# A layer norm beside a stream of scattered writes: four VectorE operations of 128x1792, each written as seven of 128x256

## The reference, cut to what matters

```
x0  = first layer: out[r] = sum over edges (r, c) of x[c] * norm(r, c)
x   = layernorm(x + x0)                       # the norm in question
xw  = einsum('ni,rih->rnh', x, W)             # 8 relations, for the second layer
layernorm(v) = (v - mean(v)) / sqrt(var(v) + 1e-5)   over the 64 features
```

## Time and profile before

| | us |
|---|---|
| median of 3 runs | 6556.67 |
| lowest, highest | 6533.79, 6564.7 |
| the profiled execution | 6601.09 |
| its span | 6599.3 |
| share of the span that DVE is busy, whole program | 35% |
| share for POOL | 43% |

### The profile page before, as it was taken

One profiled execution on the slowest core, in us unless ns is written; L12 is line 12 of the kernel. 1 busy time (PEld: TensorE's weight loads), 2 busy tenths in 40 slices (PEclk: granted clock), 3 DMA queues, 4 the chain that ended last, 5 costly groups with the idle time before them and its releaser, 6 DMA issues. The chain is left out here.

```text
span 6599.3 us, 74663 instructions
## 1 busy us (share of the span) xinstructions
PE 4016.7 (61%) x20669; PEld 3196.6 (48%) x20669; DVE 2306.5 (35%) x4709; ACT 1303.5 (20%) x2394; POOL 2863.7 (43%) x2799
## 2 busy tenths in 40 slices
PE   2333362567666642666189888878971668616687
PEld 2112111566422222666189555676751558416686
DVE  6444491234565620114511011243540113401136
ACT  0000000001343410001111222344530001300025
POOL 0655506664366666660400566000126661266602
PEclk9656575555666765555555888999985555755569
DMA  2000041111455531113633333363431112511136
GB/s 96 2 2 2 11 139 32 39 44 41 154 211 205 214 107 29 45 46 133 241 103 106 90 86 89 125 185 142 180 123 25 45 45 84 198 29 45 45 114 227
DMA packets 236073, 639.42 MB, mean 97 GB/s; under 512 B 75772, under 2 KB 77025, under 8 KB 220247
## 3 DMA queue, kind: packets, MB, share of 16 engines
q1 hardware_dynamic: 95223, 478.17, 20.1%
q0 software_dynamic: 87808, 66.01, 5.5%
q10 hardware_dynamic: 52704, 90.93, 3.7%
HBM read 324.53 MB, written 323.19 MB: 98 GB/s over the span
## 5 line engine op out<-in xcount | busy, mean ns | idle before, releaser
L1020 PE MATMUL e_ring<-e_msgs,e_hot 128*128 x6272 | 1413.7, 414 | 1081.2 <-issue 1064.8
L1020 PEld LDWEIGHTS e_ring<-e_msgs,e_hot 128*128 128x128 f32 x6272 | 1381.2, 329 | 1116.6 <-issue 1116.3
L898 POOL DMA_INDIRECT e_msgs<-y,index_D x784 | 741.5, 946 | 633.6 <-issue 453.9
L950 DVE TENSOR_TENSOR e_hot<-e_nodes,keys_D 128x2048 f32<-128x2048 f32 x147 | 336.9, 2292 | 1610.1 <-remote 884.5
L1166 POOL DMA_INDIRECT m_far<-x,index_S x392 | 373.9, 954 | 543.1 <-PE m_p_t L72 356.5
L1058 ACT COPY e_stage<-e_ring 128x512 f32<-128x512 f32 x196 | 114.9, 586 | 2458.3 <-remote 1434.6
L634 POOL DMA_INDIRECT list_D<-d_place,d_target x392 | 448.3, 1144 | 340.6 <-DVEq L588 225.2
L634 POOL DMA_INDIRECT list_S<-s_place,s_target x392 | 387.0, 987 | 436.3 <-DVEq L588 320.9
L898 POOL DMA_INDIRECT e_msgs<-y,index_S x392 | 402.7, 1027 | 364.3 <-DVE index_S L936 177.2
L898 POOL DMA_INDIRECT e_msgs<-x_by_relation,index_D x392 | 374.2, 955 | 214.6 <-issue 112.7
L1320 PE MATMUL m_ring<-m_region,m_hot 128*128 x1568 | 343.3, 423 | 60.5 <-issue 60.5
(11 more groups left out here) (361 smaller groups left out, 6329.6 us busy)
## 6 DMA issues: line engine op xcount, KB each, us to landing
x_by_relation<-d_stage SPq DMA_DIRECT2D x98, 1024.0 KB
agg<-e_stage ACTq DMA_DIRECT2D x196, 256.0 KB
n_in<-agg SPq DMA_DIRECT2D x42, 896.0 KB, 5.5
n_in<-x SPq DMA_DIRECT2D x42, 896.0 KB, 5.3
x<-n_out SPq DMA_DIRECT2D x28, 896.0 KB, 3.6
m_keyrow<-keys_by_step SPq DMA_DIRECT2D x49, 512.0 KB
messages<-m_region SPq DMA_DIRECT2D x98, 256.0 KB
m_region<-messages SPq DMA_DIRECT2D x49, 512.0 KB, 4.0
```

The costliest lines, as they stand in the source:

```text
L898: pool.indirect_dma_start(out=msgs[:, (i % HELD) * D:(i % HELD + 1) * D], out_offset=None, in_=source, in_offset=bass.IndirectOffsetOnAxis ...
L950: nc.vector.tensor_tensor(hot[g % 2][:, :, :], bc(nodes[:, 0:P].unsqueeze(1), [P, GS, P]), bc(order["keys"][:, g * GS:(g + 1) * GS].unsque ...
L1020: mm = nc.tensor.matmul(ring[:, bass.ds(bucket, D)], hot[g % 2][:, k, :], msgs[:, bass.ds(tile, D)], start=False, stop=False, skip_group_c ...
```

## The change

Each of the four operations of the norm with two tensor operands runs over all 28 nodes of a partition. It is now seven instructions, each over four nodes (128x256). The waits stand before the first, the signal is on the last. The two reductions, `hots`, the copies and everything on other engines stay as they are.

```diff
+        pieces = [slice(n * QUAD, (n + 1) * QUAD) for n in range(UQ)]
...
-                    nc.vector.tensor_tensor(value[:, :, :], got_a[h][:, :, :],
-                                            bc(K["dis"][:, c * CH:(c + 1) * CH].unsqueeze(2), [P, CH, D]), ALU.mult
-                                            ).then_inc(s_v, 1)
+                    for p in pieces:
+                        op = nc.vector.tensor_tensor(value[:, p, :], got_a[h][:, p, :],
+                                                     bc(K["dis"][:, c * CH:(c + 1) * CH][:, p].unsqueeze(2), [P, QUAD, D]),
+                                                     ALU.mult)
+                    op.then_inc(s_v, 1)
...
-                    nc.vector.tensor_tensor(value[:, :, :], value[:, :, :], got_x[h][:, :, :], ALU.add
-                                            ).then_inc(s_value, 1)
+                    for p in pieces:
+                        op = nc.vector.tensor_tensor(value[:, p, :], value[:, p, :], got_x[h][:, p, :], ALU.add)
+                    op.then_inc(s_value, 1)
...
-                    nc.vector.tensor_tensor(cent[:, :, :], value[:, :, :], bc(mean[:, :].unsqueeze(2), [P, CH, D]),
-                                            ALU.subtract).then_inc(s_c, 1)
+                    for p in pieces:
+                        op = nc.vector.tensor_tensor(cent[:, p, :], value[:, p, :],
+                                                     bc(mean[:, p].unsqueeze(2), [P, QUAD, D]), ALU.subtract)
+                    op.then_inc(s_c, 1)
...
-                    nc.vector.tensor_tensor(result[h][:, :, :], cent[:, :, :],
-                                            bc(rstd[:, :].unsqueeze(2), [P, CH, D]), ALU.mult).then_inc(s_done, 1)
+                    for p in pieces:
+                        op = nc.vector.tensor_tensor(result[h][:, p, :], cent[:, p, :],
+                                                     bc(rstd[:, p].unsqueeze(2), [P, QUAD, D]), ALU.mult)
+                    op.then_inc(s_done, 1)
```

## The result

| | before | changed |
|---|---|---|
| median, us | 6560.68 (6533.79 to 6590.12, 4 runs) | 6636.97 (6614.68 to 6641.81, 4 runs) |
| ratio of the runs, changed to before, 95% interval | | 1.0116 [1.009, 1.0143] |
| the profiled execution: its span | 6599.3 | 6612.9 |

A forecast was written before the change was run, and what follows sets the result against it. No engine was full on average; VectorE was on the path in some two fifths of the steps, GpSimd ahead. Chunk 0's 1.6 us plus 10.4 us for steps 0 and 1 made 12.0, on 6556.67: 6569 us, range 6546 to 6592.

The forecast's parts named there:

- the one on the puts: GpSimd's puts, held less, gain 35 us; all falls into its wait for L588, so nothing counted, bounds nothing and 35.
- step 6: Before each chunk's loose half: VectorE's 7.34 us idle before its copy hides the 0.40; nothing counted, at most 5.2 us.
- The line for a piece: VectorE start to start: 1.04 ns an element plus 0.067 us an instruction, so 0.333 us for 256 elements.
- 22.5 us more on VectorE: Seven pieces take 0.40 us more than one operation, over 56 operations; 12.0 us of it counted on the path.
- The sum's lower end, 0: Low end of the 12.0 us on the path, if the DMA would have held the stage anyway; upper end 22.4.
- chunk 0: First chunk, almost wholly in the dense head of 32 us: 4 x 0.40 = 1.6 us, all paid.
- Rival 1: A put takes the port from VectorE's next piece for 0.84 us: 50 us more, 6619 us; chance 0.04.
- Rival 2: No overlap on VectorE: each piece costs its whole 0.42 us, 30 us on the path, 6587 us; chance 0.05.
- Rival 5: VectorE doesn't let go between pieces, so puts wait for the whole series; same time as forecast, sharing its 0.68.
- Rival 3: Added VectorE time vanishes because DMA and stores set the dense half: 0 to 2 us, 6557 us; chance 0.18.
- Rival 4: GpSimd's puts pace something without a profile: up to 35 us back against 12, 6534 us; chance 0.05.
- the tail of the forecast: The forecast's own slow end, over 6589 us, one part of the 0.07 given to slower by over 0.5%.

The follow-up runs named there:

- e1: The kernel before, with GpSimd waiting for all 14 targets before its first put, so the norm runs without puts beside it; span 6859.7 us, one run.
- e4: The kernel before with each of the four operations replaced by a one-operand reduction of the same length, which holds no put; 6637.8 us, ratio 1.0124.
- e2: The changed kernel, with GpSimd waiting for all 14 targets before its first put, so no puts run beside the norm; span 6875.9 us, one run.
- e7: The kernel before with every eighth put waiting until the put ahead of it has landed; ratio to before 1.0065.
- e3: The kernel before with six one-column memsets ahead of each of the 56 whole operations, puts held as before; 6559.04 us, ratio 1.0005.

## Why the prediction was wrong

The step that failed is the one on the puts: "All of it falls into its wait for L588 ... I take nothing for the gain. Bounds: nothing, and 35 us". It bounds what an unheld stream of puts does by what it could give. That it could take something had no bound, though the rows asked for one: the "remote" waits behind step 6 were set down as a cause "on TensorE's side", and used as a cover, without asking what made a matmul's reader wait 7 us and more for something recorded as finished. e1 shows that they come from the puts: none is left until the puts begin. e4 shows that with the holds gone and nothing added they grow from 404 to 552 us and the whole loss of 1.2% is there; in the changed kernel they are 536.

- What bounds the kernel: that GpSimd is ahead of VectorE was right in the rows, and the conclusion that its speed is free was wrong. On the chips with late signals the puts' stream is what slows the norm, 31.7 to 45.7 us a chunk.
- The line for a piece: 0.333 us from start to start, right (2.44 us a series). 22.5 us more on VectorE, of which 12 on the path: the runs show 7 us where no put runs beside it (e1, e2). Beside the puts no run has it alone, but e4, which has none of it, loses as much as the change (1.0124 against 1.0116). It is not where the time went. The sum's lower end, 0, also leaves out the 1.6 us of chunk 0 that the list calls paid.
- The puts' durations: mean forecast about 1050, measured 1016; maximum under 2100, measured 2320, and it is the 1372 comparison that holds it (started at 1775.58, 0.10 us ahead of the put). GpSimd's wait for L588: 30 us more forecast, 108.7 measured. This row alone would have told that the forecast was off.
- Rival 1 (a put takes the port from a piece) is refuted: no piece over 429 ns. The Trainium skill (SBUF — State Buffer, Who interferes with whom) calls the pair an exclusive lock. No row here shows a put that keeps it from a piece. Rival 2 is refuted by 2.44 against 2.94. The Trainium skill's (N+151)/0.96 (VectorE: DVE Perf Modes, The TRN2 errata) gives by estimate 424 ns for a piece. The trace agrees with 419, but the pieces overlap, 0.333 us from start to start. Rival 5 is refuted by the puts' mean.
- Rival 3 (hidden whole) had no term for a loss from the puts; as to VectorE's added work e4 speaks for it. Rival 4 (the puts pace something, up to 35 us back) had 0.05, and is what happens on the other chip, where the 45 us of hold come back as 40.
- The chance of slower by over 0.5% was put at 0.07, and stood on rivals 1 and 2 and the tail of the forecast; none of them has the cause that the runs showed.

Not settled: what makes TensorE's signals late. Measured are these: a rest at every eighth put leaves 50 us of the waits, one at every 14th 374, and two open puts in place of eight leave none; it is over 3 to 4 us after a unit's last put; two of three chips have it. Through what it goes is not shown. That a hold helps because signals catch up during it is argued from e1, e4 and e7. The plainer reading, that puts started less often disturb less, is not separated from it, since every run that held or rested the puts also slowed them. A kernel with longer holds than before wasn't tried.

## What to carry to other kernels

A put issued from GpSimd that is held by VectorE is also a put that isn't disturbing anyone; before freeing it, see what it runs beside, and count a loss as well as a gain. An idle engine whose wait ends by "remote", behind an operation that the trace has as finished long ago, is no cover but an open question; the cheapest test is to run the suspected stream alone, behind the work (e1). Separate what an edit adds from what it releases by one kernel each (e3, e4), and run on more than one chip before the sign is believed.

## What the runs showed of the hardware

- Chips differ in more than speed: the same program takes 6551 to 6604 us on two chips and 5359 to 5363 on a third, and the sign of this change differs with them.
- On two of the three chips, while indirect DMAs go out one each 1.27 us beside the norm, readers of TensorE's results start up to 17 us behind the recorded matmul. Without the puts a chunk takes 31.7 us in place of 45.7 (e1), at a clock of 0.86 in place of 0.71.
- TensorE itself isn't late in seeing the others: it starts 0.05 us behind the cast that it waits for (1957.22 and 1957.27 in the changed kernel).
- A put begun during a two-operand VectorE operation ends 0.84 us behind it, gets in between two such operations, and slows neither (pieces of the first operation at 415 to 427 ns with puts beside them, at 414 to 427 in e2 without).
